# Edges sorted by weight block into 25 buckets, their sums kept in PSUM at register addresses

## The chip, the cores and the metric

One Trainium2 chip, one core. The metric is the device time of one execution in microseconds (us); the time of a kernel is the median of its runs. Engines are named as the profile names them: PE is TensorE (its weight loads are PEld), DVE is VectorE, ACT is ScalarE, POOL is GpSimd, SP is SyncE. A "q" behind a name is the engine's sequencer.

## What is computed

A graph network of two layers over 625 nodes with 1024 features and 10625 edges, all in float32. Each layer adds to `x` a graph part and a linear-attention part of the normalized features, and then a mixture of experts. The change concerns the graph part of the first layer and the attention that runs beside it:

```python
support  = xn @ W                                   # 625 x 1024
messages = support[src] * edge_weight[:, None]      # 10625 edges
gnn = segment_sum(messages, dst, num_segments=625)
x = x + gnn + mix0(xn)                              # mix0: linear attention, num * z
```

The kernel computes the segment sum as a product with a dense matrix: A[src, dst] is the sum of the weights of the edges from src to dst, and gnn is the transpose of A times support.

## The kernel before

**Precision.** A float32 operand is split into a high part (an fp32r copy, made by ACT) and a low part (what is left, made by DVE with `lo_of`), and a product is three matmuls: high x high, high x low, low x high (`mm3`). Weights arrive in 128x1024 tiles (`wr`, `wk`) by SP's DMAs in a fixed order; `a_high` makes their high parts and `v_low` their low ones, into a ring of two pairs of buffers (`ws0`, `ws1`), so a tile's high part waits for the product of the tile two before it.

**Order.** Each engine has one program written out by hand. TensorE's is: `t_features` (the products of `Wk`, then the transposes of the normalized x), `t_mix0` (the `kf` products, `Wq`, `xk`, `qf`, the two halves of `W0`, which give support, then the eight `WvT` products into four banks named `kv`, then a few 100-column matmuls `zs`), `t_adjacency` (the matrix A, with the ten `num` products of the attention among its chunks), and `t_spread` (A transposed times support, bank by bank, added to x). DVE's `v_features` also sorts: from `src` it computes the block of 125 sources that an edge belongs to (5 buckets), `v_buckets` makes one-hot rows of bucket by edge, `v_rank` a running count over them, `v_ends` and `v_placed` the place of each edge, `v_positions` sums over the buckets, `v_index` turns the place into an index `widx`. POOL's `p_sort` then scatters the edges with 85 indirect DMAs into HBM in that order, each bucket padded to whole groups, and loads the result as `se`, 128 edges x 96 chunks x (source within its block, target, weight, type). `v_groups` computes for each group of 3 chunks the block it belongs to, as an offset `off`. It stands in DVE's program behind the layernorm and ahead of the low parts of `Wq`.

**The matrix A** is made chunk by chunk, 128 edges at a time. POOL makes `lc`, the one-hot of the sources within their block (128 x 128); ACT multiplies it by the high and low parts of the weights (`lh`, `ll`, 4 of each in a ring); DVE makes `od`, the one-hot of all 628 targets. TensorE multiplies: two halves of 314 columns, for `lh` and for `ll`, so four matmuls a chunk. After the three chunks of a group DVE adds the two banks to the block of `Aw` in SBUF that a register says (`v_adjacency`). At the end ACT and DVE split `Aw` into `aw_h` and `aw_l` for `t_spread`.

**PSUM** has eight banks; `Banks.take` hands them out in order, and a product into a bank waits until its former content has been read. A register load (`reg_load`) and a register's use (`snap`) are instructions of the sequencer of the engine.

Of the kernel before, what the change touches and what calls it, by code (L numbers as in the profile page):

```python
# [3 lines left out]
ALU = mybir.AluOpType  # L4
# [11 lines left out]
NT, H = 628, 314  # L16
# [4 lines left out]
NCB = NW // 2  # L21
NR, NH, NS = 6, 3, 6
# [8 lines left out]
NSTEP = len(STEPS)  # L31
S2 = 2 * TP
# [212 lines left out]
class Program:  # L245
    def __init__(self, nc, a, out):
# [4 lines left out]
        self.d_wedges = nc.dram_tensor("scr_wedges", (128 * NW, 4), F32).ap()  # L251
# [14 lines left out]
        self.ident, self.iota = m["cst"][:, 0:128], m["cst"][:, 128:128 + NT]  # L266
        self.weights()
        self.summed_at = {SUM0 + c * (SUM1 - SUM0) // NW: c for c in range(NW)}
        self.regs = [nc.alloc_register(mybir.EngineType.DVE, f"adj{i}") for i in range(8)]

    def memory(self, nc):
# [50 lines left out]
        at("Aw", R2, T * NT)  # L324
        pair("aw", R2 + 12576, 3140)
        for i in range(14):
            at(f"od{i}", U + i * 2528 if i < 5 else R2 + 12576 + (i - 5) * 2528, NT, F32R)
        for i in range(12):
            at(f"lc{i}", U + 16736 + i * 512 if i < 7 else R2 + 37696 + (i - 7) * 512, 128, BF16)
        for i in range(4):  # L330
            for j, n in enumerate(("lh", "ll")):
                at(f"{n}{i}", U + 12640 + (2 * i + j) * 512, 128, F32R)

        at("wsoh", R2, T * EC, BF16)
        at("wssc", R2 + 864, T * EC, BF16)
        at("wst", R2 + 2592, T * EC)
# [101 lines left out]
        small("cst", 128 + NT)  # L438
# [16 lines left out]
        at("none", B, NW * 4)  # L455
        at("se", B, NW * 4)
        pair("sw", B + 1984, NW)
        at("off", B + 2752, NG, I32)
        at("n32", B + 2880, T, I32)
# [231 lines left out]
    def sync(self, e):  # L691
# [8 lines left out]
        for c in self.W.all:  # L700
            if c.key == ("Wk", 6):
                for i, j in ((0, 128), (176, 128 + NT)):
                    e.dma_start(m["cst"][:, i:j], a["cst"][:, i:j]).then_inc(*self.landed("cst_all").up(0))
# [182 lines left out]
    def t_features(self, q):  # L886
        self.t_count(q, "weighted", T, self.m["wssc"])
# [74 lines left out]
    def v_features(self, q):  # L962
# [14 lines left out]
        for j in range(2, T):  # L977
            q.wait_ge(S)
            stt(e, blk, srcf, float(TP * j), blk, ALU.is_ge, ALU.add).then_inc(*S.up("blk"))
        dat = m["dat"][0:TP, :].rearrange("p (c f) -> p c f", f=4)  # L980
# [7 lines left out]
        self.v_buckets(q, T, blk, "wsoh")  # L988
        self.v_rank(q, "weighted", 0, T, "wsoh", "wssc")
# [19 lines left out]
        self.v_groups(q, end, m["o2"][0:1, 0:NG], m["off"][0:1, :], NT, "off")  # L1009
# [49 lines left out]
    def v_groups(self, q, end, at, off, unit, key):  # L1059

        e, S = q.e, self.s("sorted")
        iota = self.iota[0:at.shape[0], 0:NG]
# [3 lines left out]
        for b in range(1, T - 1):  # L1066
# [16 lines left out]
    def v_positions(self, q, name, nb, pos):  # L1083
        st = self.m[{"weighted": "wst", "related": "st1"}[name]][0:TP, 0:nb * EC]
        q.wait_ge(self.s("sorted"))
# [48 lines left out]
    def p_sort(self, q):  # L1134
# [3 lines left out]
        e.dma_start(wedges, m["none"][:, 0:NW * 4]).then_inc(*self.landed("no_edges").up(0))  # L1138
# [204 lines left out]
    def t_mix0(self, q):  # L1343
# [34 lines left out]
        self.t_nat(q, "W0", 0, KD, self.Tt, last=lambda: self.t_count(q, "related", T, m["ssc"]))  # L1378
        self.t_nat(q, "W0", 1, KD, self.Tt)
        bs = ps.take("kv", 4)  # L1380
        for emptied in ps.before("kv"):
            q.wait_ge(*emptied)
        for k in range(KD):
# [6 lines left out]
            ins.then_inc(*self.s("product").up(("WvT", k)))  # L1390
        b, = ps.take("zs", 1)
# [41 lines left out]
    def a_mix0(self, q):  # L1433
# [1977 lines left out]
```

## Time and profile before

| | |
|---|---|
| time, three runs | 2568.77, 2576.22, 2576.75 us; median 2576.22 |
| profiled execution | 2568.9 us, of which the span shown is 2567.1 |
| mean granted TensorE clock over the span | 0.993 |
| PE busy | 2467.5 us, 96% of the span |
| DVE busy | 1793.2 us, 70% |
| ACT busy | 1422.8 us, 55% |
| POOL busy | 629.6 us, 25% |

Read it so: the times in the rows below are counted from the start of the span. A matmul's row covers it from its start to its modelled end, so rows of matmuls that follow each other overlap, and what one costs is the distance between starts. The sorting and the matrix A lie in the first 280 us; the rest is the experts and the second layer, which the change doesn't touch.

### The profile page before, as it was taken

To read this page: it belongs to the slowest core of one execution; us is meant where nothing else is said; L and a number is where in the kernel's file an instruction comes from. 1 tells how busy PE (TensorE), PEld (TensorE's weight loads), DVE (VectorE), ACT (ScalarE), POOL (GpSimd) and SP (SyncE) were. 2 spreads that over 40 slices of the span, in tenths; PEclk is the share of its full clock that TensorE was granted. 3 is DMA by queue.
4 is the path that set the end of the run, shared out by engine and by line. 5 is a ranking of instruction groups with operands and counts; after the bars stand their busy time and mean duration, and the time that the engine had idled before them with its cause. 6 is when DMAs were issued, how large, how long until landed. Compare 5 with 4: busy or idle time off the path is not lost.

```text
span 2567.1 us, 32943 instructions
## 1 busy us (share of the span) xinstructions
PE 2467.5 (96%) x12900; PEld 2025.7 (79%) x12900; DVE 1793.2 (70%) x1984; ACT 1422.8 (55%) x1894; POOL 629.6 (25%) x538
## 2 busy tenths in 40 slices
PE   7999899999999999999999999999999999999999
PEld 6978798777777777776677777777999986777797
DVE  7449655778777888778868876555456568887453
ACT  5337423666667766667753334433656658885131
POOL 5848215323221000000011004442000005656000
PEclk9999999999999999999999999999999999999999
DMA  6334027999999999999985445444211137885212
GB/s 171 80 103 119 9 92 228 315 326 323 339 321 331 326 329 328 327 329 363 344 277 154 131 138 158 122 132 112 69 50 42 33 106 255 279 284 158 98 55 73
DMA packets 166918, 502.58 MB, mean 196 GB/s; under 512 B 29814, under 2 KB 42619, under 8 KB 166764
## 3 DMA queue, kind: packets, MB, share of 16 engines
q1 hardware_dynamic: 117340, 412.38, 46.6%
q0 software_dynamic: 34928, 74.92, 10.5%
q10 hardware_dynamic: 14496, 13.17, 1.6%
q8 instruction: 103, 1.69, 0.3%
q14 instruction: 51, 0.42, 0.1%
HBM read 455.86 MB, written 44.32 MB: 195 GB/s over the span
## 4 chain that ended last, share of the span: by engine, by line
PE 75%; DVE 11%; DMA 6%; ACT 4%; issue 3%; POOL 1%; SPq 0%; DVEq 0%; ACTq 0%
PE ps L204 73%; DMA er<-in_wd 4%; DVE es_l L229 3%; ACT es_h L747 2%; DVE od L221 2%; DVE Aw L217 1%; DVE x L217 1%; DMA er<-in_wg 1%; DMA scr_ei<-xn,sdi 1%; DMA wk<-in_Wk 1%; PE ps L1974 1%; DVE ua L217 1%; PE ps L1189 1%; POOL scr_ei L2167 0%; DMA yg<-scr_eo,sgi 0%
## 5 line engine op out<-in xcount | busy, mean ns | idle before, releaser
L229 DVE TENSOR_TENSOR es_l<-er,es_h 128x1408 fp32r<-128x1408 f32 (+1 forms) x455 | 653.7, 1446 | 181.2 <-ACT es_h L747 176.3
L747 ACT ACTIVATE es_h<-er 128x1408 fp32r<-128x1408 f32 (+1 forms) x455 | 563.1, 1242 | 249.5 <-PE ps L204 169.5
L747 ACT ACTIVATE ws_h<-wr 128x1024 fp32r<-128x1024 f32 (+1 forms) x113 | 118.8, 1053 | 201.5 <-PE ps L204 190.9
L229 DVE TENSOR_TENSOR ws_l<-wr,ws_h 128x1024 fp32r<-128x1024 f32 (+1 forms) x111 | 139.3, 1255 | 118.1 <-ACT ws_h L747 112.3
L204 PE MATMUL ps<-es_h,xe_h 128*98 128x512 f32 (+1 forms) x768 | 207.9, 379 | 10.4 <-DVE es_l L229 10.2
L204 PE MATMUL ps<-es_l,xe_h 128*98 128x512 f32 (+1 forms) x768 | 204.6, 374 | 0.0
L204 PE MATMUL ps<-es_h,xe_l 128*98 128x512 f32 (+1 forms) x768 | 204.6, 374 | 0.0
L2173 POOL DMA_DIRECT2D xin<-scr_ei x16 | 9.4, 590 | 640.7 <-PE ps L1949 625.2
L204 PEld LDWEIGHTS ps<-es_h,xe_h 128*98 128x98 f32 x768 | 119.4, 163 | 57.1 <-DVE es_l L229 18.4
L204 PEld LDWEIGHTS ps<-es_h,xe_l 128*98 128x98 f32 x768 | 125.0, 163 | 38.2
L204 PEld LDWEIGHTS ps<-es_l,xe_h 128*98 128x98 f32 x768 | 125.0, 163 | 38.1
L204 PE MATMUL ps<-T_h,ws_h 128*128 128x314 f32 x656 | 151.9, 311 | 0.8 <-DVE ws_l L229 0.7
L204 PE MATMUL ps<-T_l,ws_h 128*128 128x314 f32 x656 | 149.6, 308 | 0.0
L2285 POOL DMA_INDIRECT gr<-scr_y,gidx x96 | 125.7, 1309 | 97.0 <-PE ps L204 76.7
L2978 POOL DMA_INDIRECT wrow<-scr_inv,gdst x96 | 110.3, 1149 | 154.7 <-DVE B_l L229 93.1
L204 PE MATMUL ps<-T_h,ws_l 128*128 128x314 f32 x640 | 144.5, 307 | 0.0
L204 PE MATMUL ps<-es_h,heT_h 128*98 128x512 f32 x352 | 117.0, 414 | 15.8 <-DVE es_l L229 12.0
L204 PE MATMUL ps<-ws_h,T_h 128*125 128x512 f32 x320 | 127.5, 398 | 0.0
L204 PE MATMUL ps<-ws_h,T_l 128*125 128x512 f32 x320 | 126.6, 396 | 0.0
L204 PE MATMUL ps<-ws_l,T_h 128*125 128x512 f32 x320 | 126.6, 396 | 0.0
L225 DVE SCALAR_TENSOR_TENSOR gl<-gr,gw,gh 128x1024 fp32r<-128x1024 f32 x96 | 120.4, 1278 | 8.6 <-ACT gh L2248 8.5
L1158 POOL DMA_INDIRECT scr_edges<-dat,idx x85 | 119.4, 1404 | 25.9 <-issue 25.9
(477 smaller groups left out, 6093.3 us busy)
## 6 DMA issues: line engine op xcount, KB each, us to landing
er<-in_wg SPq DMA_DIRECT2D x128, 704.0 KB
er<-in_wu SPq DMA_DIRECT2D x128, 704.0 KB
er<-in_wd SPq DMA_DIRECT2D x176, 512.0 KB
B<-in_rel SPq DMA_DIRECT2D x56, 512.0 KB
scr_y<-y SPq DMA_DIRECT2D x40, 448.0 KB
wr<-in_Wqkv SPq DMA_DIRECT2D x24, 512.0 KB
wr<-in_gate SPq DMA_DIRECT2D x16, 512.0 KB
wr<-in_w SPq DMA_DIRECT2D x13, 512.0 KB
```

Source lines behind the costliest of these rows:

```text
L204: return e.matmul(out, l, r, start=start, stop=stop, skip_group_check=True)
L217: return e.tensor_tensor(out, x, y, op)
L221: return e.tensor_scalar(out, x, s1, s2, op0) if op1 is None else e.tensor_scalar(out, x, s1, s2, op0, op1)
L225: return e.scalar_tensor_tensor(out=out, in0=x, scalar=s, in1=y, op0=op0, op1=op1)
L229: return e.tensor_tensor(lo, src, hi.bitcast(F32), ALU.subtract)
L747: q.e.activation(c.hi, c.at, ACT.Copy).then_inc(*self.s("high").up(c.key))
L1158: q.e.indirect_dma_start(self.d_edges, to, self.m["dat2"][0:TP, 4 * c:4 * c + 4], None).then_inc(*self.landed("edges").up(c))
L1189: ins = e.transpose(ps.one(bs[k // 4], 128, (k % 4) * TP, TP), buf[t][:, k * 128:(k + 1) * 128], self.ident[0:TP, 0:TP])
L1974: ins = q.e.transpose(ps.one(bs[f // 4], 128, (f % 4) * C0, C0), self.m["eh"][0:C0, f * 128:(f + 1) * 128], self.ident[0:C0, 0:C0])
L2173: e.dma_start(m["xin"][0:C0, :], self.ei[x * C0:(x + 1) * C0, :]).then_inc(*self.landed("tokens").up(x))
L2285: e.indirect_dma_start(m[f"gr{c % NR}"], None, self.d_y[:, :], of).then_inc(*self.landed(f"rows{c % NR}").up(c))
L2978: e.indirect_dma_start(m["wrow"][:, c * 8:(c + 1) * 8], None, self.d_inv[:, :], of).then_inc(*self.landed("row_weights").up(c))
```

## The change

The edges are sorted by the block of the source and of the target: 5 x 5 = 25 buckets, each padded to whole chunks of 128 (108 chunks at most). A chunk then adds to one block of 125 x 125 alone. All 25 blocks stand in seven PSUM banks, four to a bank, at 128 columns each; TensorE reads the place of each chunk's block from a register and adds there, two matmuls of 126 columns a chunk. The banks are first zeroed by matmuls with a row of zeros. `Aw` in SBUF, its clearing and its 32 additions are gone. DVE makes targets of 128 columns, and for every third chunk the weighted one-hots of the sources too; POOL and ACT make those of the other two. Rings hold 36 chunks, and the one-hots of the first 32 are made among the `WvT` products.

```diff
+NA, NB, NQ = 108, T * T, 36
+NREG = 27
+FIRST = ((0, 0), (0, 0), (0, 5), (5, 10), (10, 15), (15, 20), (20, 26), (26, 32))
...
 def v_features(self, q):
+        ts(e, bk, dstf, float(TP), None, ALU.is_ge).then_inc(*S.up())
+        for j in range(2, T):
+            q.wait_ge(S)
+            stt(e, bk, dstf, float(TP * j), bk, ALU.is_ge, ALU.add).then_inc(*S.up())
...
-        e.tensor_copy(dat[:, :, 1], dstf)
+        stt(e, dat[:, :, 1], bk, -float(TP), dstf, ALU.mult, ALU.add).then_inc(*S.up())
+        q.wait_ge(S)
+        stt(e, bk, bk, float(T), blk, ALU.mult, ALU.add).then_inc(*S.up())
...
-        self.v_buckets(q, T, blk, "wsoh")
-        self.v_rank(q, "weighted", 0, T, "wsoh", "wssc")
+        self.v_buckets(q, NB, bk, "wsoh")
+        self.v_rank(q, "weighted", 0, NB, "wsoh", "wssc")
...
-        end, base = self.v_ends(q, "weighted", T, 128 * GC, "wssc")
-        self.v_placed(q, "weighted", 0, T, base)
-        self.v_positions(q, "weighted", T, bk)
-        self.v_index(q, bk, w_, NW, m["widx"], "widx")
+        end, base = self.v_ends(q, "weighted", NB, 128, "wssc")
+        self.v_placed(q, "weighted", 0, NB, base)
+        self.v_positions(q, "weighted", NB, bk)
+        self.v_index(q, bk, w_, NA, m["widx"], "widx")
...
-        self.v_groups(q, end, m["o2"][0:1, 0:NG], m["off"][0:1, :], NT, "off")
+        self.v_groups(q, end, m["lg2"][0:1, 0:NA], m["off"][0:1, :], 128, "off")
...
 def v_groups(self, q, end, at, off, unit, key):
-        for b in range(1, T - 1):
+        for b in range(1, end.shape[1] - 1):
             q.wait_ge(S)
             stt(e, at, iota, end[:, b:b + 1], at, ALU.is_ge, ALU.add).then_inc(*S.up())
...
 def v_positions(self, q, name, nb, pos):
+        while nb > T:
+            n = nb // 2
+            q.wait_ge(S)
+            tt(q.e, st[:, 0:n * EC], st[:, 0:n * EC], st[:, (nb - n) * EC:nb * EC], ALU.add).then_inc(*S.up())
+            nb -= n
...
 def t_mix0(self, q):
+        ps.next = 7
         self.t_nat(q, "W0", 1, KD, self.Tt)
+        ps.next = 4
         bs = ps.take("kv", 4)
...
+        ps.next = 0
         b, = ps.take("zs", 1)
...
 def a_mix0(self, q):
         for k in range(KD):
             self.a_high(q, ("WvT", k))
+            self.a_adjacency(q, *FIRST[k])
...
 def v_mix0(self, q):
         for k in range(KD):
             self.v_low(q, ("WvT", k))
-            if k < T:
-                q.wait_ge(self.s("product"), ("W0", 1, 3))
-                e.memset(m["Aw"][0:TP, k * NT:(k + 1) * NT], 0.0).then_inc(*self.s("zeros").up("Aw"))
...
+            if k == 1:
+                self.v_edge_weights(q)
+            for c in range(*FIRST[k]):
+                self.v_targets(q, c)
...
+    def by_itself(self, c):
+        return c % 3 == 2
...
+    def t_zero(self, q, b):
+        for sig, key in self.zeroed_over[b]:
+            q.wait_ge(sig, key)
+        q.wait_ge(self.s("row_of_zeros"), 0)
+        for i in range(2):
+            mm(q.e, self.ps.one(b, TP, i * 256, 256), self.m["oneb"][0:1, 0:TP], self.m["zrow"][0:1, :].bitcast(BF16), True, True)
...
 def t_adjacency(self, q):
+        ps.held = set(range(7))
+        A = ps.ps[0:TP].rearrange("p b n -> p (b n)")
+        for c in range(NA):
+            if c % NREG == 0:
+                q.wait_ge(self.s("sorted"), "off")
+                e.reg_load(self.places, m["off"][0:1, c:c + NREG])
+            if c % 4 == 0 and c < 28:
+                self.t_zero(q, c // 4)
+            q.wait_ge(self.s("targets"), c)
+            to = A[:, bass.ds(e.snap(self.places[c % NREG], min_val=0, max_val=(NB - 1) * 128), TP + 1)]
+            for j, n in enumerate(("lh", "ll")):
+                if not self.by_itself(c):
                     q.wait_ge(self.s("sources_weighted"), (("high", "low")[j], c))
+                ins = mm(e, to, m[f"{n}{c % NQ}"][:, 0:TP], m[f"od{c % NQ}"][:, 0:TP + 1], False, j == 1)
+            ins.then_inc(*self.s("chunk").up(c))
+            if c % 12 == 11 and c // 12 < 8:
+                self.t_num(q, c // 12 // T, c // 12 % T)
+        self.t_num(q, 1, 3)
+        ps.held, ps.next = set(), 0
+        self.t_num(q, 1, 4)
...
 def v_targets(self, q, c):
+        if self.by_itself(c):
+            q.wait_ge(self.s("edge_weights"), "low")
+            for n, w in (("lh", "sw_h"), ("ll", "sw_l")):
+                ts(q.e, m[f"{n}{c % NQ}"], self.iota, src, m[w][:, c:c + 1].bitcast(F32), ALU.is_equal, ALU.mult)
+        ts(q.e, m[f"od{c % NQ}"], self.iota, dst, None, ALU.is_equal).then_inc(*self.s("targets").up(c))
...
 def v_adjacency(self, q):
+        for g in range(NA // 12):
+            for c in range(32 + 12 * g, min(44 + 12 * g, NA)):
+                if g and c == 32 + 12 * g + 6 and g < 9:
+                    self.v_num(q, (g - 1) // T, (g - 1) % T)
                 self.v_targets(q, c)
-            tt(e, o, ps.two(ps.group["weight", g][0], slice(0, TP)), o, ALU.add).then_inc(*ps.out(("weight", g)))
...
 def a_spread(self, q):
+        for b in range(7):
+            hi, _, src = self.summed_weights(b)
+            q.wait_ge(self.s("chunk"), NA - 1)
+            e.activation(hi, src, ACT.Copy).then_inc(*self.s("A_high").up(b))
...
 def v_spread(self, q):
+        for b in range(7):
+            hi, lo, src = self.summed_weights(b)
+            q.wait_ge(self.s("A_high"), b)
+            lo_of(e, lo, src, hi).then_inc(*self.s("A_low").up(b))
+            if b in (2, 4):
+                self.v_num(q, 1, 3 + b // 4)
```

`summed_weights(b)` gives the blocks of bank b: their places in `aw_h` and `aw_l`, and the bank itself as the source. POOL's loop over `lc` now has 24 buffers, leaves out every third chunk, and starts after the `xk` products.

## Rows read from the trace of the kernel before

**Rows 1.** Timeline of PE: start us, us, then what ran.
```profile
195.80 0.27 PE L204 MATMUL ps<-ones,qf_l 128*125 128x100 f32 x1
...
197.77 0.27 PE L204 MATMUL ps<-ones,qf_l 128*125 128x100 f32 x1
...
244.24 0.45 PE L204 MATMUL ps<-od,lh 128*125 128x314 f32 x2
...
249.22 0.45 PE L204 MATMUL ps<-od,ll 128*125 128x314 f32 x2
```
**Rows 2.** Chain of work that ended last, 0 to 340 us: start us, us.
```profile
51.26 121.87 PE ps L204 x770
...
276.79 28.06 PE ps L204 x120
```
**Rows 3.** Busy time by stretch: PE, PEld, DVE, ACT, POOL; clock, DMA, GB/s.
```profile
240.00:260.00 20.00, 18.93 (x121) 17.35 (x120) 20.00 (x37) 18.15 (x61) 19.73 (x23) 1.00 0.00 1
```
**Rows 4.** Operations on od, Aw and lc: duration ns min/median/max.
```profile
L221 DVE TENSOR_SCALAR od<-cst,se x96: 529/561/682, 193.7 to 269.7; 128x628 fp32r<-128x628 f32 x96
...
L217 DVE TENSOR_TENSOR Aw<-ps,Aw x32: 792/793/811, 204.9 to 274.2; 125x628 f32 x32
...
L1626 POOL TENSOR_SCALAR lc<-cst,se x96: 591/819/1479, 163.0 to 269.8; 128x128 bf16<-128x128 f32 x96
L1586 ACT ACTIVATE lh<-lc,sw_h x96: 385/388/423, 197.9 to 271.4; 128x128 fp32r<-128x128 bf16 x96
```
**Rows 5.** DVE's register load and register operations, and the last addition.
```profile
L1606 DVEq TENSOR_LOAD <-off x4: 593/600/2626, 200.5 to 261.2; - x4
...
L1612 DVEq FUSED_REGOPS  x32: 55/55/63, 203.1 to 274.1; - x32
...
274.22 0.81 DVE L217 TENSOR_TENSOR Aw<-ps,Aw 125x628 f32 x1 [0.21 <-DVE Aw L217]
```
**Rows 6.** Timeline of DVE, first 23 us; idle before and its releaser in brackets.
```profile
5.54 0.82 DVE L225 SCALAR_TENSOR_TENSOR blk<-srcf,blk 125x85 f32<-125x85 f32 x3
...
7.12 0.61 DVE L217 TENSOR_TENSOR wsoh<-cst,blk 125x425 bf16<-125x425 f32 x1
7.77 1.05 DVE L1021 TENSOR_TENSOR_SCAN wssc<-oneb,wsoh 125x425 bf16<-125x425 bf16 x1
...
13.98 1.23 DVE L229 TENSOR_TENSOR ws_l<-wk,ws_h 128x1024 fp32r<-128x1024 f32 x1 [1.19 <-ACT ws_h L747]
...
17.43 0.60 DVE L217 TENSOR_TENSOR wst<-wssc,pr 125x425 f32<-125x425 bf16 x1
...
18.71 0.96 DVE L1086 TENSOR_REDUCE bk<-wst 125x85 f32<-125x425 f32 x1
...
22.76 1.23 DVE L229 TENSOR_TENSOR ws_l<-wk,ws_h 128x1024 fp32r<-128x1024 f32 x1 [1.80 <-ACT ws_h L747]
```
**Rows 7.** Timeline of POOL, the first seven lc tiles.
```profile
163.00 4.09 POOL L1626 TENSOR_SCALAR lc<-cst,se 128x128 bf16<-128x128 f32 x7 [2.23 <-DMA se<-scr_wedges]
```
**Rows 8.** Costliest groups of the whole run: the high parts of 1024 columns.
```profile
L747 ACT ACTIVATE ws_h<-wr 128x1024 fp32r<-128x1024 f32 (+1 forms) x113 | 118.8, 1053 | 201.5 <-PE ps L204 190.9
```
**Rows 9.** Timeline of PE in the first 28 us.
```profile
12.94 0.55 PE L204 MATMUL ps<-proj_h,ws_h 128*128 128x256 f32 x1 [3.52 <-DVE ws_l L229]
...
24.04 0.39 PE L204 MATMUL ps<-proj_h,ws_h 128*128 128x256 f32 x1 [2.99 <-DVE ws_l L229]
...
24.83 0.41 PE L204 MATMUL ps<-proj_h,ws_l 128*128 128x256 f32 x1
...
27.60 0.41 PE L204 MATMUL ps<-proj_h,ws_h 128*128 128x256 f32 x1
```
**Rows 10.** Timeline of DVE and PE around the first Wq product.
```profile
58.71 0.81 DVE L225 SCALAR_TENSOR_TENSOR o<-cst,lg,o 1x32 f32<-1x32 f32 x3
...
62.81 0.42 DVE L225 SCALAR_TENSOR_TENSOR hx<-ps,hx 125x256 f32<-125x256 f32 x1 [0.49 <-ACT hx L1426]
...
65.53 0.28 PE L204 MATMUL ps<-proj_h,ws_h 128*128 128x256 f32 x1
```

More of the change, by code:

```diff
@@ L269, in __init__ @@
         self.regs = [nc.alloc_register(mybir.EngineType.DVE, f"adj{i}") for i in range(8)]
+        self.places = [nc.alloc_register(mybir.EngineType.PE, f"place{i}") for i in range(NREG)]
     def memory(self, nc):
@@ L436, in spair @@
             small(name + "_l", n, F32R)
-        small("cst", 128 + NT)
+        small("cst", 256)
+        small("off", NA, I32)
         at("tri", R2 + 27232, 128)
@@ L454, in memory @@
         at("rwp", B, 1024, F32R)
[L455 to L459, printed above, removed]
+        at("none", B, NA * 4)
+        at("se", B, NA * 4)
+        pair("sw", B + 1984, NA)
+        at("n32", B + 2880, NB, I32)
         at("widx", B + 3040, EC, I32)
@@ L1545, in v_mix0 @@
         e.reciprocal(nrm, nrm).then_inc(*self.s("over_sum").up(0))
-        for c in range(7, 14):
-            self.v_targets(q, c)
+        for i in range(4):
+            c = slice(i * 512, (i + 1) * 512)
+            q.wait_ge(*ps.done("kv", i, "high"))
+            lo_of(e, m["kv0_l"][:, c], ps.one(ps.group["kv"][i]), m["kv0_h"][:, c]).then_inc(*ps.out("kv", i, "low"))
     def v_num(self, q, h, t):
@@ L1580, in a_adjacency @@
+        self.t_num(q, 1, 3)
+        ps.held, ps.next = set(), 0
+        self.t_num(q, 1, 4)
+    def a_adjacency(self, q, a=32, b=NA):
+        e, m = q.e, self.m
+        for c in range(a, b):
+            if self.by_itself(c):
+                continue
+            lc, lh, ll = m[f"lc{self.unweighted(c) % 24}"], m[f"lh{c % NQ}"], m[f"ll{c % NQ}"]
             q.wait_ge(self.s("sources"), c)
             q.wait_ge(self.s("edge_weights"), "low")
-            if c < 4:
-                q.wait_ge(self.s("sorted"), "goff")
-            else:
-                q.wait_ge(self.s("chunk"), c - 4)
+            q.wait_ge(self.s("product"), ("W0", 1, 3))
+            if c >= NQ:
+                q.wait_ge(self.s("chunk"), c - NQ)
@@ L1589, in v_targets @@
     def v_targets(self, q, c):
[L1590 to L1591 removed]
+        m = self.m
+        if c < NQ:
             q.wait_ge(self.s("product"), ("W0", 1, 3))
         else:
[L1594 to L1614 removed]
@@ L1650, in a_spread @@
         e, m = q.e, self.m
-        for t in range(T):
-            q.wait_ge(*self.ps.done(("weight", NG - 1)))
-            e.activation(self.by_targets("aw_h", t), self.by_targets("Aw", t), ACT.Copy).then_inc(*self.s("A_high").up(t))
+        for b in range(7):
+            hi, _, src = self.summed_weights(b)
+            q.wait_ge(self.s("chunk"), NA - 1)
+            e.activation(hi, src, ACT.Copy).then_inc(*self.s("A_high").up(b))
         self.a_high(q, ("om", 0))
```

137 lines of the change are left out of this document (54 added, 83 removed).

## The prediction

> **What bounds the kernel now.** I read the page's header first, then a table of busy time by stretch, then the groups of one tile, and last the timelines and the chain of waits around the two places that the diff touches: the first 70 us, and the stretch that builds the matrix of summed edge weights.
>
> The stretch runs from the last of the 100-column matmuls (the last starts at 197.77 [rows 1]) to the first matmul of the spreading at 276.79 [rows 2]: I count 78.9 us. In its middle the table shows DVE busy 20.00 of 20 us, with TensorE at 18.93 and the granted clock at 1.00 [rows 3]. A busy TensorE isn't a full one here, since a matmul's row is longer than its spacing; I count spacings. DVE's own work is what ends last: 96 one-hot tiles `od` of 628 columns at about 0.56 us and 32 additions into `Aw` at 0.79 [rows 4]; the last one, at 274.22, waits for the one before it and for nothing else [rows 5].
>
> TensorE's own work in it is 384 matmuls of 314 columns and 60 of 512. The 512-column ones cost 0.234 us each (28.06 us for 120 [rows 2]): 14.0 us. The 314-column ones, where nothing holds them up, are 34 from the start at 244.24 to that at 249.22, 0.146 us each [rows 1]: 56 us. So TensorE would need 70 of the 78.9 us by itself. Relieving DVE alone would be worth 9 us; the change cuts both.
>
> **The stretch after.** A chunk has two matmuls of 126 columns in place of four of 314. No such matmul stands in the trace; the nearest has 125 rows of weights and 100 columns: 18 steps from 195.80 to 197.77 give 0.109 us each [rows 1]. At 1 column per 1/2.4 ns, 100 columns are 42 ns and 126 are 53 ns, so something other than columns sets that spacing (a new set of weights for each), and I take 0.109 for 126 columns too. 216 of them: 23.5 us. The Trainium skill, page "TensorE: Matmul & The Clock Gate", section "Back-to-back issue gap", gives about 81 ns for a pair of weight load and 128-column matmul; this trace's row says 109 ns, and by the page's figure the sum would be 216 x 0.028 = 6 us lower.
>
> The address of each chunk's output comes from a register. The trace has that on DVE alone: one register operation of 55 ns for each of the 32 additions, and an addition that waits for the one before it starts 0.21 us after its end [rows 5]. Two dependent DVE operations without a register lie 0.04 us apart (17.43, two of 0.60, then 18.71 [rows 6]). So a register address costs up to 0.17 us where nothing covers it. On TensorE the queue runs ahead of the array, so from below it costs nothing (a chunk takes 2 x 0.109 = 0.22 us); from above each of the two matmuls pays the whole 0.21 (0.42 us a chunk). I take the 55 ns of the register operation as laid bare once for each chunk: 0.27 us, the lower end being nearer because matmuls with waits between them run without gaps in the stretch of before. 108 chunks: 29.5 us (23.5 to 45.4).
>
> Beside them: the same 60 matmuls for `num`, 14.0 us; 14 zeroing matmuls of 256 columns at 0.118 (256 columns at 2.4 GHz are 107 ns, and the 314 and 512 column rows lie 15 to 21 ns above their columns; I take 11): 1.7 us; four register loads. A load of eight registers takes 0.6 us [rows 5]; of 27 it may take 0.6 to 2.0, the first is covered by the matmuls ahead of it: 1.8 us (0 to 8). Then the end: the chain "five additions, ACT copy, DVE subtraction" goes, and two `num` products (2.8 us, counted above) cover the first ACT copy and DVE subtraction out of PSUM: 0.1 us bare. Sum 29.5 + 14.0 + 1.7 + 1.8 + 0.1 = 47.1 us, against 78.9: **31.8 us less**.
>
> Is it TensorE that sets it? DVE has 76 chunks left of 108, 76 `od` and 25 pairs of weighted one-hots, 126 operations of 128 columns. From 425 elements in 0.61 and 1024 in 1.23 us an element costs 1.035 ns and an operation 0.17 [rows 6]: 0.30 us for 128 columns, at most 38 us in all, and seven more for ten `x` updates. ACT has 51 chunks left at two operations of 0.388 us [rows 4], at most 40 us and less with their overlap. Both lie under 47. GpSimd makes 72 `lc` tiles at 0.59 to 0.82 us [rows 4]: 43 to 59 us, but it starts when the sorted edges land, before the `WvT` products, not at this stretch. It started at 163.00 [rows 7]; later by 12 us it is at 175, and done by 234 at the latest, about 20 us before TensorE would be.
>
> In the `WvT` part ACT gets 22 chunks (17 us at most) beside eight high parts of 1.05 us [rows 8], in 22 us. The fullest steps come to 3.4 us against TensorE's 2.8; two or three such steps and the slack of one buffer make 0.5 us (0 to 3).
>
> **The front.** Here the change adds, and I price it from DVE's own rows [rows 6]. Ahead of the scan: four more bucket operations (0.27 each by the three in 0.82) and one more product, 1.4 us; the bucket one-hots at 2125 elements instead of 425, 1700 x 1.035 ns = 1.8 us; the scan, 1.05 us at 425, whose element costs (1.05 - 0.17)/425 = 2.07 ns, 3.5 us more. That is 6.7 us before the low parts of `proj` and `Wk` can be made, and TensorE's first matmul at 12.94 [rows 9] waits for those. Behind them, ahead of `widx`: two operations of `v_placed` at 1.8 more each, three folding additions of 1020, 510 and 255 elements (1.23 + 0.70 + 0.43 and gaps, 2.5), the reduction over 340 rather than 425 elements (-0.2), wider small operations 0.3: 6.1 us. In all 12.8.
>
> Not all of it arrives. DVE waited 1.19 us at 13.98 and 1.80 at 22.76 for high parts that came late with their loads [rows 6]; those waits are filled: 12.8 - 3.0 = 9.8 us at the latter row. DVE's queue behind it may have a little more slack to give, and the two-buffer ring of `Wk` (TensorE's product, ACT's copy, DVE's subtraction) may take it back. I take 9.4 us (8 to 11) at the point where TensorE becomes dense, 51.26: from there the chain is TensorE alone for 121.87 us [rows 2], and no slack takes anything back. GpSimd's scatter of 85 DMAs moves with `widx` by 11.6 us, and ends ahead of its readers as said above.
>
> Then `v_groups`. Now one comparison and three more on 32 columns (0.81 us for the three [rows 10]); after, 23 more on 108 columns at about 0.29: 5.8 us more, in the DVE queue ahead of `v_low(Wq,0)` and of the first `kf` piece. TensorE needs both for the first `Wq` product: the weights, and the bank of the first `kf`, which `elu_sum` empties at 62.81 + 0.42 [rows 10]. That product began at 65.53 [rows 10]; with 5.8 us more the bank is free at 69.1: 3.6 us. After an idle of 2.99 us TensorE's clock fell, and 13 spacings of 256 columns took 24.83 to 27.60, 0.213 us each, the 1.2 GHz level [rows 9], against 0.12 warm; some 16 of those cost 1.5 us. The same is due here: 1.3 us. Sum of the front **14.3 us**, 11 to 18.
>
> **Total.** -31.8 + 0.5 + 14.3 = -17.0 us. On the profiled execution's 2568.9 that gives 2551.9. The median shown is 2576.2, with two runs there and one at 2568.8; midway between the two levels the base is 2572.5, and the forecast 2555.5. A difference under 0.3% (7.7 us) is about what a measurement here can't tell from none.
>
> **Rivals.** (B) The sequencer sets the chunk: each register-addressed matmul pays 0.21 us, 0.42 a chunk, 108 x 0.15 = 16.2 us more than my sum: net -0.8, about 2572. For it: the 0.21 on DVE; against it: TensorE's queue. Chance 0.17.
> (C) The other side: the array empties at each register operation. Then a chunk pays one full matmul row (0.27 us [rows 1]), the 0.21 bare [rows 5] and 0.109: 0.59 us, 34.6 us more, net +17.6, about 2590. It decides from 0.43 us a chunk up, and makes it slower by over 0.3% from 0.50. Nothing in the trace shows such emptying, nor excludes it. Chance 0.12.
> (D) The front is cheaper than counted, since DVE's new work displaces waits for loads that end by 30 us: 5 us instead of 14.3, net -26, 2546. Against it stands the dense chain from 51.26. Chance 0.09.
> (E) TensorE, whose array works half the time in this stretch, falls to 1.2 GHz. The weight-bound chunks keep 0.109 (105 ns of columns), but 60 `num` matmuls of 512 columns double: 60 x 0.2 + 1.6 = 13.6 us, net -3.4, 2569. [...] The clock in the stretch of before is 1.00 [rows 3], with matmuls 2.5 times as wide. Chance 0.05.
> (F) ACT falls behind in the `WvT` part: without overlap its full steps are 4 x 0.78 + 1.05 = 4.2 us against 2.8 [rows 4, 8], and six steps cost about 6 us: net -11, 2561. Chance 0.04.
> The forecast keeps 0.53, its own range 2545 to 2566. Faster: the forecast and D nearly whole, and a third of B, E and F: 0.69. Slower: C and some of B: 0.14. Same: 0.17. For 8 in 10 the range reaches from D's near side, 2543, to past B with the higher base, 2580.
>
> **What would show it.** After: `lh`/`ll` matmuls of 126 columns in pairs, chunk starts 0.22 to 0.30 us apart (B: 0.42, C: near 0.6); register operations on TensorE's sequencer, 108 of 55 ns; DVE no longer full from the last 100-column matmul on, and that stretch near 47 us; `widx` some 12 us later; dense TensorE from 60.7 rather than 51.26; TensorE idle some 3.6 us ahead of the first `Wq` product, and slow matmuls behind it. The prediction is wrong if the chunk cost passes 0.35 us, or the front's shift exceeds 18 us.

## The result and the profile after

The kernel after takes 2593.05 us (median of 5 runs, 2590.03 to 2598.71), the kernel before 2576.75 in the 5 runs beside them: a ratio of 1.0069, 95% interval 1.0053 to 1.0086, so 16.3 us or 0.7% slower. The forecast was 2555.5 with a range of 2543 to 2580. The profiled execution of after took 2590.03 us (span 2588.2, clock 0.981; before 0.993 over 2567.1).

Two marks, as in [rows 1, 2], cut the difference of the two traces into parts: the stretch runs from the last 100-column matmul to the first spreading matmul.

| | before | after | difference | forecast |
|---|---|---|---|---|
| last 100-column matmul starts | 197.77 | 215.19 | +17.4 | +14.8 |
| the stretch after it | 79.0 | 77.8 | -1.2 | -31.8 |
| first spreading matmul starts | 276.79 | 292.99 | +16.2 | -17.0 |

So in these two traces the new stretch is about as long as the old one, and what came ahead of it makes up the whole difference. The timeline of PE of the kernel after answers to [rows 1]:

```profile
215.19 0.27 PE L207 MATMUL ps<-ones,qf_l 128*125 128x100 f32 x1
219.91 0.65 PE L207 MATMUL ps<-zrow,oneb 1*125 1x256 bf16 x2 [4.44 <-issue]
...
243.14 0.46 PE L207 MATMUL ps<-od,lh 128*125 128x126 f32 x1 [4.74 <-issue]
243.40 0.41 PE L207 MATMUL ps<-od,ll 128*125 128x126 f32 x1
243.61 0.41 PE L207 MATMUL ps<-od,lh 128*125 128x126 f32 x1
...
250.69 0.27 PE L207 MATMUL ps<-od,lh 128*125 128x126 f32 x1
...
252.55 0.27 PE L207 MATMUL ps<-od,ll 128*125 128x126 f32 x1
...
259.35 0.46 PE L207 MATMUL ps<-od,lh 128*125 128x126 f32 x1 [3.82 <-DVE od L224]
```

Two things stand in it. From 250.69 to 252.55 there are 17 steps of 0.109 us: the register-addressed matmuls run exactly as fast as those of 100 columns in [rows 1]. But TensorE stands idle ahead of groups of them, and behind an idle the steps are 0.21 us. Its chain of work that ended last shows the four idles, and what TensorE waits for in them:

```profile
207.48 8.00 PE ps L207 x44
215.68 4.23 issue
219.91 18.07 PE ps L207 x76
239.89 3.25 issue
243.14 7.44 PE ps L207 x28
258.43 0.92 issue
259.35 11.18 PE ps L207 x66
270.53 4.56 issue
275.09 45.92 PE ps L207 x198
```

```profile
L1594 PEldq TENSOR_LOAD <-off x4: 6366/6378/9177, 213.4 to 268.5; - x4
...
L1598 PEldq MOVE  x72: 29/29/37, 219.9 to 287.0; - x72
L1598 PEldq FUSED_REGOPS  x36: 50/50/50, 220.3 to 287.4; - x36
```

Of the four register loads, of 27 places each, three take 6.4 us and one 9.2. The queue ahead covers about 2 to 4 us of each; the rest is the four idles, 4.44, 4.74, 3.82 and 4.56 us: 17.6 us. The third is put down to DVE's `od`, which is the semaphore wait behind the load; the load itself (252.7 to 259.1) is what was late. The register operations are one for each of the 108 chunks on this line, and 72 more in the helper of the matmuls (37 ns). Busy time by stretch between the idles (PE, PEld, DVE, ACT, POOL; clock, DMA, GB/s), to hold against [rows 3]:

```profile
220.00:238.40 18.40, 18.40 (x80) 14.28 (x80) 11.09 (x44) 10.32 (x34) 10.60 (x16) 0.63 0.97 275
243.14:255.50 12.36, 12.36 (x66) 11.36 (x66) 9.18 (x37) 9.06 (x30) 3.81 (x6) 0.70 0.00 1
259.35:270.50 11.15, 11.15 (x66) 10.20 (x66) 8.26 (x32) 7.33 (x24) 0.00 (x0) 0.78 0.01 3
275.09:292.99 17.90, 17.90 (x78) 15.86 (x79) 3.73 (x6) 2.85 (x7) 0.00 (x0) 0.64 0.00 1
```

DVE, ACT and POOL are no longer full, as forecast. But the clock, 1.00 in the stretch of before, is 0.63 to 0.78 while TensorE works, between its two levels of 1.2 and 2.4 GHz. (1 - clock) x length over the four rows is 6.8 + 3.7 + 2.5 + 6.4 = 19.4 us. So 77.8 = 17.6 of idles + 19.4 of low clock + 40.8 of work at full clock.

The front, on DVE's timeline, to hold against [rows 6, 10]:

```profile
5.00 0.82 DVE L228 SCALAR_TENSOR_TENSOR bk<-dstf,bk 125x85 f32<-125x85 f32 x3
...
6.98 2.38 DVE L220 TENSOR_TENSOR wsoh<-cst,bk 125x2125 bf16<-125x2125 f32 x1
9.39 4.59 DVE L1031 TENSOR_TENSOR_SCAN wssc<-oneb,wsoh 125x2125 bf16<-125x2125 bf16 x1
...
21.10 2.37 DVE L220 TENSOR_TENSOR wst<-wssc,pr 125x2125 f32<-125x2125 bf16 x1
...
25.92 2.40 DVE L220 TENSOR_TENSOR wst<-wst 125x1020 f32<-125x1020 f32 x3
28.36 0.73 DVE L1103 TENSOR_REDUCE bk<-wst 125x85 f32<-125x340 f32 x1
...
30.29 1.22 DVE L232 TENSOR_TENSOR ws_l<-wk,ws_h 128x1024 fp32r<-128x1024 f32 x1
...
66.13 8.44 DVE L228 SCALAR_TENSOR_TENSOR lg<-cst,lg,lg 1x108 f32<-1x108 f32 x23
```

The low part that ran at 22.76 now runs at 30.29: 7.5 us later, where 9.8 were forecast. Not all of the gap is an error of the forecast: `edge_type` was waited for 1.67 us in the trace of before and 0.25 in this one, ahead of everything that the change adds, so this front started 1.5 us early. PE in the same kernel becomes dense at 58.63, not 51.26, and its first `Wq` product comes at 78.37, not 65.53:

```profile
58.63 0.35 PE L207 MATMUL ps<-g_h,T_h 128*125 128x256 f32 x1 [0.78 <-DVE T_l L232]
...
78.37 0.58 PE L207 MATMUL ps<-proj_h,ws_h 128*128 128x256 f32 x1 [5.29 <-DVE hx L228]
```

### The profile page after: what moved, and what is told of

Same layout as the page of the kernel before. It is cut to its first block, busy times and chain, and to the rows that moved or that the text cites. A ratio compares the mean times of both kernels' runs of the same rounds, so it can differ in the third digit from the quotient of the medians.

```text
span 2588.2 us, 32642 instructions
## 1 busy us (share of the span) xinstructions
PE 2456.3 (95%) x12746; PEld 2011.9 (78%) x12746; DVE 1779.5 (69%) x2061; ACT 1407.6 (54%) x1848; POOL 606.8 (23%) x514
## 3 DMA queue, kind: packets, MB, share of 16 engines
q8 instruction: 102, 1.67, 0.3%
## 4 chain that ended last, share of the span: by engine, by line
PE 74%; DVE 10%; DMA 8%; ACT 4%; issue 3%; POOL 1%; ACTq 0%; DVEq 0%; SPq 0%; POOLq 0%
PE ps L207 72%; DMA er<-in_wd 4%; DVE es_l L232 3%; ACT es_h L750 2%; DMA gr<-scr_y,gidx 1%; DMA er<-in_wg 1%; DMA scr_ei<-xn,sdi 1%; DVE ws_l L232 1%; DVE x L220 1%; PE ps L2023 1%; PE ps L1206 1%; POOL scr_ei L2216 0%; ACT ws_h L750 0%; DMA yg<-scr_eo,sgi 0%; DVE ua L220 0%
```

## The experiments

The theories. **L**: the four loads stop TensorE, and the low clock follows from the stops. **W**: matmuls of few columns let the clock fall by themselves. **R**: register operations pace the chunks. **F**: DVE's front reaches the end in full. Each row's stretch runs from the last 100-column matmul to the first spreading one, with the mean clock over it, both from the profiled execution. "Low" is (1 - mean clock) x span over the whole kernel, as a mean over all its runs, with its standard error: the time that a clock below full takes (part of an idle counts in it: some 4.5 us for the four of the kernel after). The ratio is to the kernel before, with its 95% interval; "one" is a single execution.

| kernel | us | ratio | stretch | clock in it | low, us |
|---|---|---|---|---|---|
| before | 2573.49 | | 79.0 | 1.00 | 21.9 ± 0.7 |
| after | 2593.05 | 1.0069 (1.0053 to 1.0086) | 77.8 | 0.69 | 51.3 ± 1.7 |
| e1 | 2564.46 | 0.9963 (0.9945 to 0.9982) | 47.9 | 0.93 | 34.4 ± 1.8 |
| e2 | 2567.73 | one | 56.3 | 0.82 | 35.9 |
| e3 | 2568.92 | one | 54.5 | 0.78 | 38.5 |
| e4 | 2580.57 | one | 67.9 | 0.75 | 36.1 |
| e5 | 2550.45 | 0.9893 (0.9863 to 0.9924) | 53.1 | 0.81 | 31.2 ± 1.2 |
| e6 | 2589.61 | 1.0059 (1.0037 to 1.0080) | 79.2 | 0.66 | 53.4 ± 1.2 |
| e7 | 2570.72 | 0.9986 (0.9967 to 1.0005) | 53.4 | 0.84 | 37.8 ± 1.7 |
| e8 | 2562.87 | 0.9948 (0.9930 to 0.9967) | 56.4 | 0.79 | 35.6 ± 1.3 |
| e9 | 2556.36 | 0.9937 (0.9920 to 0.9954) | 50.2 | 0.93 | 25.8 ± 1.0 |
| e10 | 2569.80 | 0.9979 (0.9962 to 0.9996) | 62.3 | 0.75 | 37.2 ± 0.9 |
| e11 | 2592.41 | 1.0072 (1.0044 to 1.0100) | 75.5 | 0.77 | 44.5 ± 1.4 |
| e12 | 2570.79 | 0.9986 (0.9966 to 1.0005) | 50.3 | 0.86 | 37.3 ± 1.7 |

The experiments ran in four groups, each on another chip with the kernel before beside it: e1, e3, e4, e5; e2, e6, e7, e8; e9, e10, e11; e12. Its medians in them lay between 2572.96 and 2574.74, 2576.75 beside the kernel after, and the row has those of e9 to e11. Its "low" was 22.2, 22.7, 21.9 and 21.8 us, each within about 1, so "low" can be compared from group to group.

A mark of one trace is less sure than it looks. In the eight kernels with all of the new front (after, e1 to e4, e7, e11, e12) the last 100-column matmul starts anywhere from 214.7 to 220.4 us, 217.2 in the mean; in the four with the comparisons moved (e6, e8, e9, e10) from 207.9 to 210.1; in before and e5 at 197.8 and 199.7.

### e1: places known when the kernel is built

```diff
-            if c % NREG == 0:
-                q.wait_ge(self.s("sorted"), "off")
-                e.reg_load(self.places, m["off"][0:1, c:c + NREG])
...
-            to = A[:, bass.ds(e.snap(self.places[c % NREG], ...), TP + 1)]
+            u = c * NB // NA * 128
+            to = A[:, u:u + TP + 1]
```

> The changed kernel with every chunk's block at a fixed place and no register load or register operation on TensorE (the sums land in the wrong blocks). Theory L (the four register loads stop TensorE for 17.6 us in all, and the stops let its clock fall to 1.2 GHz, which costs the other 21 of the 77.8 us): the stretch from the last 100-column matmul to the first of the spreading falls to 39 to 42 us at a granted clock of 1.00, and the time by about 37 us against the changed kernel, to some 2555. Rival W (the 126-column matmuls by themselves let the clock fall): the stretch only loses the 17.6 us and keeps about 60, with a clock of 0.7 to 0.8, the time about 2575. Rival R (the register operations set the pace): chunks a good deal closer than 0.22 us at full clock.

The stretch fell from 77.8 to 47.9 us, and the kernel by 28.6. The loads and registers, with what follows from them, thus cost nearly the whole of the forecast gain. Neither L (39 to 42 us at a clock of 1.00, some 2555) nor W (about 60 us, 2575) came: the result lies between them. In the table of busy time the clock is low at first and full later. There is no load to stop TensorE; the 2.1 us that it idles in the second row are waits for DVE's `x` updates:

```profile
214.70:228.70 14.00, 13.74 (x74) 10.84 (x73) 13.78 (x54) 11.11 (x38) 13.00 (x20) 0.78 1.02 295
228.70:262.50 33.80, 31.69 (x221) 27.89 (x220) 25.47 (x94) 21.61 (x70) 6.85 (x10) 0.99 0.28 79
```

At full clock its work is 14.0 x 0.78 + 33.8 x 0.99 = 44.4 us. Where the clock is low its chunks start 0.42 us apart (225.89, 226.31), without any register operation: that spacing, which was to be the sign of rival B, is the lower clock's.

### e2: the first load alone; e3: the loads without their use

e2 has `if c == 0:` in place of `if c % NREG == 0:`. e3 keeps the loads and has e1's places.

> The changed kernel with the first of its four loads alone; the 27 registers serve all 108 chunks, so register operations stay and three quarters of the blocks are wrong. Theory L: one stop of some 4.4 us ahead of the chunks, then none; the clock is low for the first part and full from there, the stretch 47 to 53 us. A rival by which the register operations cost anything: chunk starts further apart than with fixed places (0.22 us).

> The changed kernel with its four loads of 27 registers kept and every chunk's block at a fixed place (the sums land in the wrong blocks). Theory L: nothing changes, the stretch stays at 76 to 80 us with four stops of 3.8 to 4.8 us and the clock of 0.66 to 0.80. Rival R: without register operations the stretch is clearly shorter.

e2's one load took 6.47 us and left an idle of 4.53; three loads fewer gave 25.3 us, by a single execution; its stretch of 56.3 is longer than the 47 to 53 expected. e3 told nothing of loads: its trace has no TENSOR_LOAD (nobody reads the registers there, and the loads seem to have been dropped when it was built), and it is e1 once more, at 2568.92. It shows how far one profile goes: with the same instructions the clock in the stretch is 0.78 here and 0.93 in e1. Hence the column over all runs.

### e4: twelve loads of 9 registers

`NREG = 9`.

> The changed kernel with 12 loads of 9 registers for 4 of 27. If a load costs by the register (6.37 us / 27 = 0.236 each), each lasts 2.1 us, and most of it hides behind the matmuls that are queued, since 1.6 us of each long load did: twelve stops under 1 us, the stretch some 50 us or less, and the clock near 1.00. If it costs by the instruction (6.4 us each), the stretch grows by 8 x 4.6 us to over 110. If as on DVE (0.6 us for 8), each lasts under 1 us and none shows.

```profile
L1594 PEldq TENSOR_LOAD <-off x12: 841/2168/8269, 215.3 to 277.3; - x12
```

None of the three expected outcomes came. Ten of the twelve took 0.84 to 2.17 us, and nine of them were hidden; the tenth, of 2.17 at 269.2, stopped TensorE for 1.55 us. Those at 219.3 and 231.7 took 8.27 and 7.89 and stopped it for 6.66 and 5.77 us. The duration doesn't follow the number of registers alone.

### e5: e1 with the front of before

It sorts into 5 buckets again, on top of e1 (`v_buckets(q, T, blk, "wsoh")` and so on, the removed lines of the diff restored).

> As the run with fixed places, and the sort of before beside it: 5 buckets, 4 comparisons for the groups (places and targets are wrong for the product, the instructions are those of the changed kernel from the WvT products on). Theory F (the front's 25-bucket sort and its 24 comparisons delay TensorE by 17 us, all of which arrives at the end): 16 to 19 us less than the run with fixed places, some 2538, and the last 100-column matmul back at 198 to 199 us. Rival: the front's delay is mostly absorbed, under 8 us less.

2550.45 against e1's 2564.46: the front costs 14.0 us, by the marks 214.7 - 199.7 = 15.0, by the two ratios 18. Each is uncertain by some 6 us or more. F's 16 to 19 us fit, and the rival's "under 8" doesn't.

### e6: the 24 comparisons later

`v_groups` is cut into eight pieces of three comparisons, one behind each `xk` low part, where TensorE is dense.

> The changed kernel with the 24 comparisons of the chunks' blocks moved on DVE from ahead of the low parts of Wq to behind the low parts of xk, three after each. Theory F: TensorE's idle ahead of the first Wq product (it waits for the bank of the first kf) goes, 4 to 6 us, and with it the slow matmuls behind it, 1 to 2 us: the last 100-column matmul 5 to 8 us earlier, the time by as much lower. Rival: DVE's three operations for each xk bank hold up the xk or qf products, and nothing is gained.

The first `Wq` product has no idle, and the last 100-column matmul starts 6.3 us earlier; the medians differ by 3.4. The four loads (6.4 to 7.1 us) still stop TensorE, for 4.47, 1.55, 3.77 and 4.56 us.

### e7: four places in one word, one load

```diff
+for j in range(1, 4):
+    stt(e, at[:, 0:NREG], at[:, j * NREG:(j + 1) * NREG], float(32 ** j), at[:, 0:NREG], ALU.mult, ALU.add)
...
-self.t_nat(q, "W0", 1, KD, self.Tt)
+self.t_nat(q, "W0", 1, KD, self.Tt, last=lambda: self.t_places(q))   # the one load
...
+word = e.snap(self.places[c % NREG])
+to = A[:, bass.ds(e.snap((word >> (5 * (c // NREG))) & 0xF80, ...), TP + 1)]
```

> The whole computation: DVE packs four places of 5 bits into each of 27 words, TensorE loads them once, behind the products of the third tile of the second half of W0, and takes each place out by a shift and a mask. Theory L: the load hides behind some 7 us of queued matmuls, the stretch of the chunks is 39 to 44 us at full clock, the time 33 to 38 us below the changed kernel, about 2557. Rival R2: shift and mask cost more register operations, and set the chunk's pace above 0.22 us. Rival Q: TensorE's queue doesn't hold 7 us of matmuls, and the load stops it by 3 us or more in the W0 part.

No stop is left, the load took 2.54 us and is hidden behind the 512-column matmuls of `W0`, and the kernel is 22.3 us faster than after. That is less than the 33 to 38 expected: the stretch took 53.4 us, since its clock was 0.84 and not full, so L's half on the clock missed. Every chunk now shifts and masks as well, and the trace has 378 register operations for the 108 chunks (29 to 62 ns, the medians of its groups), where the kernel after has 180; at full clock the work is 53.4 x 0.84 = 44.9 us, e1's, without any, 44.4. R falls: register operations cost TensorE nothing visible here.

### e8: e7 and e6 together

> The packed places and the comparisons moved behind xk together; the whole computation. If both causes stand by themselves, the gains add: 5 to 8 us below the run with packed places alone, about 2550, and 20 to 30 us below the kernel before.

```profile
210.10:218.00 7.90, 7.64 (x38) 6.27 (x38) 7.67 (x29) 6.42 (x21) 7.90 (x13) 0.74 1.04 302
218.00:230.00 12.00, 12.00 (x44) 8.83 (x42) 7.37 (x28) 5.20 (x16) 5.85 (x9) 0.50 1.00 281
230.00:242.00 12.00, 12.00 (x64) 11.11 (x64) 9.64 (x39) 9.39 (x31) 5.57 (x8) 0.68 0.28 81
242.00:254.00 12.00, 11.97 (x81) 10.43 (x81) 11.71 (x48) 9.81 (x34) 0.00 (x0) 1.00 0.01 3
```

7.9 us faster than e7, as expected, and faster than the kernel before by 0.5% (0.3 to 0.7), 12 us where 20 to 30 were expected. Its only idle in the stretch is 0.26 us, and yet 24 us of it have a clock of 0.50 and 0.68; in all that is 56.4 x (1 - 0.79) = 11.8 us. Over its 12 runs "low" is 35.6 us against 21.9 before. The stops can't be the only cause of the low clock.

### e9: the same matmuls, twice as wide

```diff
-& 0xF80, ...), TP + 1)]
+& 0xF00, ...), 2 * (TP + 1))].rearrange("p (r n) -> p r n", r=2)
...
-m[f"od{c % NQ}"][:, 0:TP + 1]
+m[f"od{c % NQ}"][:, 0:TP + 1].unsqueeze(1).broadcast_to([128, 2, TP + 1])
```

> As e8 (packed places loaded once, ahead of the stretch; comparisons behind kf), but each chunk matmul reads its 126 target columns twice over and writes 252 columns, from an even block on; the sums are therefore others. The number of matmuls and of weight loads, and all waits, stay. W (few columns to a matmul are what lets the clock fall): a 256-column matmul costs 0.12 us at full clock, so 216 x 0.12 + 14.0 + 1.7 = 41.6 us, with a low start as in e1 43 to 46; mean clock in the stretch over 0.95, against 0.79 in e8; the kernel 10 us faster than e8, near 2553, though it does twice the columns. G (the clock falls for another reason, such as the waits or the weight loads themselves, and the width has no part): the mean clock stays near 0.79 and the stretch grows to 53 to 60 us; the kernel is at 2563 or above. They part at a mean clock of 0.87.

```profile
208.70:258.90 50.20, 49.94 (x294) 41.82 (x294) 39.38 (x147) 33.05 (x109) 21.73 (x32) 0.93 0.47 135
...
218.00:230.00 12.00, 12.00 (x80) 10.03 (x80) 10.48 (x43) 9.78 (x33) 10.83 (x16) 0.99 0.99 279
230.00:242.00 12.00, 12.00 (x77) 10.43 (x77) 12.00 (x50) 12.00 (x42) 1.59 (x3) 1.00 0.19 56
```

W holds against G: with twice the columns the clock is 0.99 where e8 had 0.50, 80 matmuls fit where 44 did. One profile could be chance, but over all runs "low" falls from 35.6 to 25.8 us, six times the standard error of the difference. The time falls less clearly: the median by 6.5 us, by the ratios 2.8, and their intervals overlap. The stretch is longer than the 43 to 46 us expected, and its mean clock is 0.93, not over 0.95; DVE and ACT, both full in the third row, may be a part of that, which wasn't shown.

### e10: the one load at the start of the chunks

`t_places` moves from the `W0` products to ahead of chunk 0.

> As e8, but the one load of 27 registers stands at the start of the chunks instead of in the middle of the W0 products. P (the place or what the queue holds at that time sets a load's duration): it takes 6.4 us as in the kernel after, and TensorE idles 4.5 us before the first chunk; the stretch 61 us and longer, and some us more for the clock behind the stop; the kernel near 2568 to 2572. K (the packed load is short wherever it stands): 2.5 us, an idle of at most 1 us, the kernel as e8, 2563 within 3.

```profile
L1596 PEldq TENSOR_LOAD <-off x1: 6323/6323/6323, 206.1 to 206.1; - x1
```
```profile
212.67 0.65 PE L207 MATMUL ps<-zrow,oneb 1*125 1x256 bf16 x2 [4.48 <-issue]
```

P holds: the same load of the same 27 words takes 6.32 us here and 2.54 at its place in e8. The kernel is 6.9 us slower, of which 4.5 are the idle. The clock was full ahead of the idle (steps of 0.109 up to 207.92) and low behind it: the 29 us from 213 to 242 run at 0.52, with TensorE busy throughout. But over all runs "low" is only 1.6 us above e8's, not clear of its error, for e8's narrow matmuls run slow for a time without a stop too.

### e11: the stops of after, with wide matmuls

The kernel after with e9's width (the place masked by `& 0xF00` as there).

> As the kernel after, with its four loads of 27 registers in their places, but with chunk matmuls of 252 columns as in e9. The four stops stay: 17.6 us idle in either theory. W (the few columns keep the clock low; a stop costs only its own time and some 1.3 us of slow matmuls behind it): 17.6 + 41.6 + 4 x 1.3 + 2 = 66 us for the stretch, against 77.8 in the kernel after, which makes the kernel 11 us faster than after, near 2582, and the clock outside the stops over 0.9. L (each stop of 4.5 us lowers the clock for most of a group of 27 chunks, whatever the width): clock between the stops near 0.7, the stretch 17.6 + 41.6/0.7 = 77 us or more, the kernel at 2590 or above.

```profile
243.77 0.57 PE L207 MATMUL ps<-od,lh 128*125 128x252 f32 x1 [6.04 <-issue]
244.13 0.42 PE L207 MATMUL ps<-od,ll 128*125 128x252 f32 x1
244.35 0.41 PE L207 MATMUL ps<-od,lh 128*125 128x252 f32 x1
```
```profile
220.00:230.00 10.00, 9.87 (x36) 7.84 (x36) 5.58 (x22) 5.21 (x16) 5.09 (x8) 0.50 1.02 287
```

L's number came, or nearly: 75.5 us and 2592.41, where W gave 66 and 2582; the four idles were 19.6 us in all, and the clock between them 0.70 to 0.82. So width keeps the clock up only where nothing stops. Behind a stop wide matmuls are at 1.2 GHz as well, for the 10 us of the second row. Over all runs "low" is 44.5 us against e9's 25.8. W as worded, 1.3 us of slow matmuls behind a stop, is refuted.

### e12: nine loads of 12 registers

`NREG = 12`, nothing else.

> As the kernel after, but nine loads of 12 registers in place of four of 27. Every load but the first then stands right behind a num product, whose matmuls are 512 columns wide. N (a load is quick right behind wide matmuls: in e4 the two loads that stood behind a num product took 0.84 us for 9 registers, and in e7 and e8 one among 512-column matmuls 2.54 us for 27, 0.094 us a register; elsewhere 0.236 and more): eight loads of 1.1 to 1.2 us, hidden behind the num product; no TensorE idle over 1 us in the stretch, its length 53 to 57 us, the kernel near 2571 as e7. M (0.236 us a register wherever it stands, short ones by chance): 2.8 us each with one or two long ones of 8, some idle of 0.5 to 1 us at each and 5 us at the long ones, a stretch of 66 us and more, the kernel near 2580 as e4.

```profile
L1594 PEldq TENSOR_LOAD <-off x9: 846/849/3130, 217.9 to 261.6; - x9
```

N's outcome came: one stop by a load, of 0.68 us, a stretch of 50.3 us, and a kernel 22.3 us faster than after by one constant. N's durations held for part: five took 0.85 us, but those at 223.4, 231.6 and 238.0 took 3.0 to 3.1 behind a `num` product as well. The six 512-column matmuls of the product ahead (1.4 us at full clock, 2.6 at the lower) hid the first two with what was queued beside; the third, at full clock, ended at 241.05 and was the one that stopped TensorE:

```profile
241.29 0.32 PE L207 MATMUL ps<-od,lh 128*125 128x126 f32 x1 [0.68 <-DVE od L224]
```

The loads of all these traces, set side by side, show an order that no run was made to test. Where the share of the DMA engines (the last column but one of the busy time, here taken over each load) was 0.01 or less, a load of 27 took 6.37 to 6.38 us (six loads: after, e6, e11), of 9 among chunk matmuls 2.16 to 2.17 (seven, e4), which is 0.24 us a register, and behind a `num` product 9 took 0.84 (two) and 12 took 0.85 (four, e12). Every load longer than its like fell, at least in part, while the DMA engines were busy: e4's 8.27 and 7.89 at shares of 1.04 and 0.95, e12's three of 3.0 to 3.1 at 0.91 to 1.05, and the second loads of after, e11 and e6, 9.18, 8.52 and 7.07, at 0.50, 0.46 and 0.29 in the mean. DVE's own maximum of 2.63 in [rows 5] did too, at 0.99, where its 0.60 stood at 0.16 and less. Yet the first load of after, e6, e10 and e11 and that of e2 took 6.3 to 6.5 at 0.87 to 0.90, so a busy DMA doesn't always lengthen one.

## Why the prediction was wrong

The account closes: the forecast for the stretch was 47.1 us and it took 77.8, 30.7 more, and the front with the `WvT` part brought 17.4 in place of 14.8.

- **"Four register loads ... 1.8 us (0 to 8)": the term that failed first, by 15.8 us.** It was sized from DVE's load of eight registers, 0.6 us [rows 5], which stood beside a maximum of 2.63 in the same row. On TensorE 27 registers took 6.4 us and 9.2, and stopped it for 17.6 in all. The prediction hid "the first" behind the matmuls ahead; of each of the four only 2 to 4 us were hidden. e7 and e12, where the same places reach TensorE with no stop or with one of 0.68 us, are each 22.3 us faster than after. e10 gives the price of one stop with what follows it: 6.9 us.
- **The clock: +19.4 us, which the sum set at nothing and rival E priced at 13.6 with a chance of 0.05.** Two causes work in it, and "low" shows each apart. Few columns, with no stop in either kernel: e8 35.6 against e9 25.8, 10 us. Four stops: after 51.3 against e7 and e12, 37.8 and 37.3, 14 us with narrow matmuls; e11 44.5 against e9 25.8, 19 us with wide ones (both differences hold the part of the idles themselves, some 4.5 us in after, and the second also the idle ahead of `Wq`, which e11 has and e9 hasn't). The clock of 1.00 in [rows 3] was taken as evidence against E, but it belongs to matmuls of 314 columns and to a stretch without a stop.
- **E's own step "the weight-bound chunks keep 0.109" was wrong.** At 1.2 GHz they take 0.21 us (243.40 to 243.61), so what sets them slows with the clock too. The Trainium skill, page "TensorE: Matmul & The Clock Gate", section "Why this matters for your kernels", warns of idle gaps between bursts of matmuls. This case's traces agree: in e10 the steps are 0.109 us ahead of an idle of 4.48 us and 0.21 behind it. I weighed a low clock at 1 in 20, and never asked whether the change brings such idles.
- **"0.27 us" a chunk: 0.218 measured, 29.5 - 23.5 = 6.0 us too high.** The lower bound was the truth; the register operation of 50 ns runs ahead of the array. Rival B (0.42) and rival C (0.59) are refuted by the steps of 0.109 us and by e7 against e1. C gave 2590, within 3 us of the median, by another mechanism than the real one. The Trainium skill, same page, section "Back-to-back issue gap", gives 81 ns for such a pair; this trace differs, with 109 ns at full clock.
- **The rest of the stretch, +1.5 us** (40.8 of work, where 23.5 + 14.0 + 1.7 + 0.1 = 39.3 were counted). The four rows of busy time have no idle, so it isn't in waits. The zeroing pairs cost more than their columns: in e1, at full clock, the rows below put 0.72 us between the matmul ahead of a pair and the second one behind it, where the sum had 0.45; seven pairs make 1.9 us.

```profile
217.73 0.27 PE L207 MATMUL ps<-od,ll 128*125 128x126 f32 x1
217.93 0.43 PE L207 MATMUL ps<-zrow,oneb 1*125 1x256 bf16 x2
218.29 0.32 PE L207 MATMUL ps<-od,lh 128*125 128x126 f32 x1
218.45 0.27 PE L207 MATMUL ps<-od,ll 128*125 128x126 f32 x1
```

In the kernels with no stop or a short one the work at full clock is 42 to 45 us (e3 42.5, e5 43.0, e12 43.3, e1 44.4, e8 44.6, e7 44.9), where the forecast without its load term had 45.3.

- **The dense start, 9.4 forecast, 7.4 came.** Each operation came as priced (2.38 for 2125 elements, 4.59 for the scan). Some 1.5 us of the 2.0 missing are the early `edge_type` of this one trace, and no saving by the change: in the eleven other kernels with the 25-bucket sort TensorE becomes dense at 58.3 to 61.3 us, 60.0 in the mean, 8.7 later than in before, within the range of 8 to 11. (`widx`, ready at 30.4 and not at 21.0, is 9.4 later where 11.6 were forecast, for the most part for the same reason.) Rival D has no support in them.
- **The comparisons, 3.6 forecast, 5.5 came.** They take 8.44 / 23 = 0.37 us each rather than 0.29. Behind the idle of 5.29 us the slow matmuls cost more than 1.3: some 4.6 us stand between this point and the stretch, the `WvT` part's 1.3 (0.5 forecast) among them. e6 takes the idle away for a gain of 3.4 us, e8 for 7.9 over e7, each uncertain by about 5 us; by the marks of all twelve kernels it is 217.2 - 208.9 = 8.3.
- **The front in all, 14.3 forecast, 11 to 18:** e5 against e1 has 14.0 by the medians and up to 18 by the ratios. By the mean mark of the eight kernels against e5's, which has the same `WvT` part, it is 217.2 - 199.7 = 17.5. All lie within the range; this part of the prediction was right, perhaps a few us low.
- **Right as well:** DVE is not full any more, the kernel is TensorE's alone in the stretch, GpSimd and ACT keep up, though GpSimd's last `lc` starts at 247.8 and wasn't done by 234, since it waits for ACT. (The prediction's 25 pairs on DVE and 51 chunks on ACT are 26 and 50, which changes nothing.)

What stays open. What sets a load's duration: 0.84 to 8.27 us for 9 registers in e4, 2.54 or 6.32 for the same 27 in e8 and e10. The place matters (e10), the count does where the DMA engines rest, and the long ones go with a busy DMA; whether the traffic is their cause wasn't tested. And why the low part of the clock is of such different length from run to run: e1 and e3 run the same instructions at 0.93 and 0.78. The 4.9 us by which the profiled executions differ beyond the first spreading matmul (21.1 against 16.2) weren't followed further; the medians differ by 16.3.

## What to carry to other kernels

Read every instruction of a sequencer as one that can stop its engine: its price is its duration less what is queued ahead of it, so load few registers at a time and right behind long matmuls (`NREG = 12`, behind them, was worth 22 us; `NREG = 9`, mostly not, still had 14.0 us of stops), or pack several values into a word and load once, early. When matmuls are made narrower, don't count on the clock that the wide ones had: price the stretch once at each of the two levels, with every spacing nearly doubled at the lower one (0.109 to 0.21 us, 0.234 to 0.43), and ask of each new idle of some microseconds what the matmuls behind it will cost. The version with the packed places and the comparisons moved under dense work (e8) beats both kernels: 2562.87 us, 0.5% less than before and 1.2% less than after.

## What the runs showed of the hardware

- A TENSOR_LOAD of 27 registers on TensorE took 6.3 to 9.2 us ahead of narrow matmuls and 2.54 among 512-column ones; of 12, 0.85 to 1.04 or 3.0 to 3.1; of 9, 0.84 to 8.27. With the DMA engines at rest it was 6.37 for 27 and 2.17 for 9 among narrow matmuls, and 0.84 for 9 and 0.85 for 12 right behind 512-column ones. On DVE eight took 0.6, and one of the four 2.63 [rows 5].
- Register operations of 29 to 62 ns on TensorE, 3.5 for a chunk of 0.218 us in e7, cost nothing visible.
- At 1.2 GHz a matmul of 126 columns with new weights is 0.21 us from the next, at 2.4 GHz 0.109; one of 252 columns 0.21 too. At the lower level width up to 252 columns was thus free.
- TensorE, busy without a gap, was at 0.50 for 12 us (e8, 218 to 230) with matmuls of 126 columns; with 252 it was at 0.99 over the same 12 us (e9), and at 0.50 for 10 us only behind a stop (e11).
